# Expert layers over node columns split 250 and 376 instead of 312 and 314

## What is computed

```python
logits = jnp.einsum('td,ed->te', xf, gate_w)
probs = jax.nn.softmax(logits, axis=-1)
top_w, top_i = jax.lax.top_k(probs, TOP_K)
top_w = top_w / (top_w.sum(axis=-1, keepdims=True) + 1e-09)
combine = combine.at[jnp.arange(T)[:, None], top_i].add(top_w)
h = jax.nn.gelu(jnp.einsum('td,edh->teh', xf, w1) + b1[None, :, :])
y = jnp.einsum('teh,ehd->ted', h, w2) + b2[None, :, :]
out = jnp.einsum('ted,te->td', y, combine)
```

## Time and profile before

| | |
|---|---|
| median of 3 runs | 1740.7 us (1740.62 to 1742.16) |
| span of the profiled execution | 1740.0 us |
| TensorE busy | 1682.7 us, 97% |
| VectorE busy | 931.1 us, 54% |
| ScalarE busy | 466.8 us, 27% |
| GpSimd busy | 690.3 us, 40% |
| mean granted TensorE clock | 0.988 of full |

### The profile page before, as it was taken

How to read it: one execution, slowest core, us unless ns; L and a number is a source line. 1 busy time by engine, 2 the same in 40 slices (tenths; PEclk the granted TensorE clock), 3 DMA queues, 4 the chain that set the end, 5 groups by cost and what they waited for, 6 DMA issues and landing times.

```text
span 1740.0 us, 25810 instructions
## 1 busy us (share of the span) xinstructions
PE 1682.7 (97%) x10227; PEld 1579.9 (91%) x10227; DVE 931.1 (54%) x1879; ACT 466.8 (27%) x875; POOL 690.3 (40%) x428
## 2 busy tenths in 40 slices
PE   8799999999999988899999999999999999999999
PEld 7699999997999988799377888989999999998999
DVE  8993537416866679857497554423112141225731
ACT  6443123203223138934222211101011011112310
POOL 1026865652445520060020175431644435342663
PEclk9899999999999999899899999999999999999999
DMA  2002222423212210014010022111221111110222
GB/s 90 1 28 70 73 69 65 142 78 128 64 55 64 64 56 10 1 47 143 7 43 1 11 85 64 57 45 37 73 64 55 46 51 59 55 55 30 64 73 72
DMA packets 42000, 99.84 MB, mean 57 GB/s; under 512 B 10509, under 2 KB 12143, under 8 KB 41895
## 3 DMA queue, kind: packets, MB, share of 16 engines
q1 hardware_dynamic: 37828, 87.87, 16.3%
q10 hardware_dynamic: 4066, 10.46, 1.7%
HBM read 96.39 MB, written 1.92 MB: 57 GB/s over the span
## 4 chain that ended last, share of the span: by engine, by line
PE 82%; DVE 11%; ACT 4%; issue 1%; POOL 1%; DVEq 0%; POOLq 0%; ACTq 0%
PE bank L2421 10%; PE bank L2423 10%; PE bank L2422 10%; PE banks L2421 9%; PE banks L2422 9%; PE banks L2423 9%; PE bank L2983 3%; PE banks L2983 3%; PE bank L3060 3%; PE bank L3065 3%; PE banks L3060 2%; PE banks L3065 2%; DVE tmp L1827 1%; DVE src_hot L1491 1%; PE banks L2835 1%
## 5 line engine op out<-in xcount | busy, mean ns | idle before, releaser
L833 POOL TENSOR_TENSOR w_hi<-raw,ones_r 128x768 fp32r<-128x768 f32 (+1 forms) x192 | 294.0, 1532 | 994.9 <-PE banks L2423 368.3
L836 POOL TENSOR_TENSOR w_lo<-raw,w_hi 128x768 fp32r<-128x768 f32 (+1 forms) x192 | 370.5, 1930 | 15.0
L2421 PE MATMUL bank<-w_hi,xT_hi 128*125 128x384 f32 (+2 forms) x560 | 187.8, 335 | 1.7 <-DVE small L1968 1.2
L2423 PE MATMUL bank<-w_hi,xT_lo 128*125 128x384 f32 (+2 forms) x560 | 186.7, 333 | 0.0
L2422 PE MATMUL bank<-w_lo,xT_hi 128*125 128x384 f32 (+2 forms) x560 | 186.5, 333 | 0.0
L2421 PE MATMUL banks<-w_hi,xT_hi 128*125 128x384 f32 (+2 forms) x440 | 151.8, 345 | 0.2 <-DVE xT_lo L1569 0.2
L2422 PE MATMUL banks<-w_lo,xT_hi 128*125 128x384 f32 (+2 forms) x440 | 151.4, 344 | 0.0
L2423 PE MATMUL banks<-w_hi,xT_lo 128*125 128x384 f32 (+2 forms) x440 | 151.3, 344 | 0.0
L1618 DVE TENSOR_TENSOR hT_lo<-tmp,hT_hi 128x312 fp32r<-128x312 f32 (+1 forms) x88 | 94.3, 1078 | 41.9 <-ACT hT_hi L970 41.5
L2421 PEld LDWEIGHTS bank<-w_hi,xT_hi 128*125 128x125 f32 x560 | 103.9, 186 | 5.0 <-DVE small L1968 1.4
L2422 PEld LDWEIGHTS bank<-w_lo,xT_hi 128*125 128x125 f32 x560 | 103.9, 185 | 2.5
(11 more groups left out here) (579 smaller groups left out, 3923.4 us busy)
## 6 DMA issues: line engine op xcount, KB each, us to landing
raw<-wa SPq DMA_DIRECT2D x92, 384.0 KB, 3.0
raw<-wc SPq DMA_DIRECT2D x76, 384.0 KB, 3.0
raw<-wb SPq DMA_DIRECT2D x28, 448.0 KB, 3.3
w_rows<-w_in ACTq DMA_DIRECT2D x1, 3072.0 KB, 12.6
bias<-bias_in ACTq DMA_DIRECT2D x6, 384.0 KB
w_first<-w_in ACTq DMA_DIRECT2D x1, 2304.0 KB, 11.2
w_down<-w_down_in SPq DMA_DIRECT2D x8, 288.0 KB, 5.2
w_up<-w_up_in SPq DMA_DIRECT2D x1, 2304.0 KB, 10.6
```

Of the source, the lines that this page charges most:

```text
L833: pool.tensor_tensor(w_hi[:, k, 0:width], raw[:, k, 0:width], ones[:, 0:1].to_broadcast([P, width]), ALU.mult).then_inc(S("unit_high"), 1)
L836: pool.tensor_tensor(w_lo[:, k, 0:width], raw[:, k, 0:width], f(w_hi[:, k, 0:width]), ALU.subtract).then_inc(S("unit_split"), 1)
L2421: tell_used(pe.matmul(dst, l_hi, r_hi, start=start, stop=False))
L2423: return pe.matmul(dst, l_lo, r_hi, start=False, stop=stop)
```

## The change

The expert layers get their own split of the columns: part 0 has 250 (tiles 0 and 1), part 1 has 376. The first four jobs go in the order (tile 0, part 0), (tile 1, part 0), (tile 0, part 1), (tile 1, part 1); from job 4 on they are as before. The turn of tile 4 moves from ahead of job 0 to behind it. `router(0)` waits for the low parts of two tiles, not three. `router(1)` moves from behind job 0 to behind job 1, the transposes of the logits from behind job 1 to behind job 2, f1's importance from behind job 3 to behind job 4. The transposes of the routing weights stay behind job 5. As 376 columns are more than a slot of `tmp` holds, five slots of 376 lie in its place and a sixth behind `xT_hi`. The first product of the down layer waits for four low parts, not two. g0's up layer keeps 312 and 314.

```diff
+EXPERT_CH = [(0, 2 * TN), (2 * TN, NP - 2 * TN)]
...
-IMPORTANCE = 3
+IMPORTANCE = 4
+ROUTER_JOB = 1
...
     if s == "g0" and j < 6:
         return j % 3, j // 3
+    if s != "g0" and j < 4:
+        return j % 2, j // 2
     return j // 2, j % 2
+
+
+def columns_of(s, c):
+
+    return (CH if s == "g0" else EXPERT_CH)[c]
...
     def ffn(f, tiles):
         add(f + "_routerT", 0, f + "_routerT_read", 1)
-        left_turn()
         jobs, lag = 2 * tiles, EXPERT_LAG
         for j, spread in enumerate(spread_after(jobs)):
             if j < jobs:
                 add(f + "_hidden", j, f + "_activated", j + 1)
             if j == 0:
+                left_turn()
+            if j == ROUTER_JOB:
                 add(f + "_routerT", 1, f + "_routerT_read", 2)
-            if j == 1:
+            if j == ROUTER_JOB + 1:
                 add(f + "_router", 0, f + "_routed", 1)
...
+        last_slot = at_("last_slot", [P, EXPERT_CH[1][1]], f32, XT + up32(KD * NP * 4))
...
+        expert_tmp = at_("expert_tmp", [P, TSLOTS - 1, EXPERT_CH[1][1]], f32, tmp_off)
...
+        def slot_of(s, j, cn):
+
+            k = j % TSLOTS
+            if s == "g0":
+                return tmp[:, k, 0:cn]
+            return expert_tmp[:, k, 0:cn] if k < TSLOTS - 1 else last_slot[:, 0:cn]
...
                 def router(c):
-                    c0, cn = CH[c]
-                    pe.wait_ge(*E(s + "_xT_low", (6, 2 * NT)[c]))
+                    c0, cn = EXPERT_CH[c]
+                    pe.wait_ge(*E(s + "_xT_low", (4, 2 * NT)[c]))
...
                 router(0)
-                turn_behind(s)(NT - 1)
                 jobs = 2 * tiles
                 for j, spread in enumerate(spread_after(jobs)):
                     if j < jobs:
                         up(s, j)
                     if j == 0:
+                        turn_behind(s)(NT - 1)
+                    if j == ROUTER_JOB:
                         router(1)
-                    if j == 1:
+                    if j == ROUTER_JOB + 1:
                         pe.wait_ge(*E(s + "_routerT_read", 2))
...
-                down(s + "d", s + "_down", hT_hi, hT_lo, lambda k: pe.wait_ge(*E(s + "_low", 2 * k + 2)), seed=seed,
+                down(s + "d", s + "_down", hT_hi, hT_lo, lambda k: pe.wait_ge(*E(s + "_low", max(2 * k + 2, 4))), seed=seed,
```

More of the change, by code:

```diff
@@ L593, in network @@
         tmp = at_("tmp", [P, TSLOTS, WIDE], f32, tmp_off)
+        expert_tmp = at_("expert_tmp", [P, TSLOTS - 1, EXPERT_CH[1][1]], f32, tmp_off)
+        assert (TSLOTS - 1) * EXPERT_CH[1][1] <= TSLOTS * WIDE
         iota = new("iota", [TN, NP], i16)
@@ L967, in high @@
                     m, c = job_of(s, i)
-                    c0, cn = CH[c]
+                    c0, cn = columns_of(s, c)
                     act.wait_ge(*E(full, i + 1))
-                    act.activation(hT_hi[:, m, c0:c0 + cn], tmp[:, i % TSLOTS, 0:cn], ACT.Copy
+                    act.activation(hT_hi[:, m, c0:c0 + cn], slot_of(s, i, cn), ACT.Copy
                                    ).then_inc(S(s + "_high"), 1)
@@ L976, in hidden @@
                         m, c = job_of(s, j)
-                        cn = CH[c][1]
+                        cn = columns_of(s, c)[1]
                         if made <= j - TSLOTS:
@@ L983, in hidden @@
                             act.wait_ge(*E(s + "_low", j - TSLOTS + 1))
-                        act.activation(tmp[:, j % TSLOTS, 0:cn], bank(s + "_hidden", j)[:, 0:cn], func,
+                        act.activation(slot_of(s, j, cn), bank(s + "_hidden", j)[:, 0:cn], func,
                                        **scale_bias(m)).then_inc(S(s + "_activated"), 1)
@@ L992, in expert_layer @@
                 normal_rows(s)
-                for c, (c0, cn) in enumerate(CH):
+                for c, (c0, cn) in enumerate(EXPERT_CH):
                     await_group(act, s + "_routerT", c)
@@ L1607, in hidden_low @@
                     if j < jobs and weigh:
-                        cn = CH[j % 2][1]
+                        cn = columns_of(s, job_of(s, j)[1])[1]
                         dve.wait_ge(*E(s + "_activated", j + 1))
                         await_group(dve, s + "_cB", j)
-                        TT(tmp[:, j % TSLOTS, 0:cn], tmp[:, j % TSLOTS, 0:cn], bank(s + "_cB", j)[:, 0:cn], ALU.mult
+                        TT(slot_of(s, j, cn), slot_of(s, j, cn), bank(s + "_cB", j)[:, 0:cn], ALU.mult
                            ).then_inc(S(s + "_weighted"), 1)
@@ L1615, in hidden_low @@
                         m, c = job_of(s, i)
-                        c0, cn = CH[c]
+                        c0, cn = columns_of(s, c)
                         dve.wait_ge(*E(s + "_high", i + 1))
-                        TT(hT_lo[:, m, c0:c0 + cn], tmp[:, i % TSLOTS, 0:cn], f(hT_hi[:, m, c0:c0 + cn]),
+                        TT(hT_lo[:, m, c0:c0 + cn], slot_of(s, i, cn), f(hT_hi[:, m, c0:c0 + cn]),
                            ALU.subtract).then_inc(S(s + "_low"), 1)
@@ L2613, in expert_layer @@
                     for i in spread:
-                        m, (c0, cn) = i // 2, CH[i % 2]
+                        m, c = job_of(s, i)
+                        c0, cn = columns_of(s, c)
                         q, kind = (m // 3, m % 3) if tiles == 12 else (m // 2, 2 * (m % 2))
```

## The result

| | before | after |
|---|---|---|
| median of 12 runs each | 1742.12 us (1739.72 to 1745.59) | 1744.49 us (1743.62 to 1746.97) |
| ratio to before, with its 95% interval | | 1.0018 [1.0010, 1.0026] |
| span of the profiled execution | 1740.0 us | 1744.6 us |
| time of the profiled execution | about 1741.7 us (its span plus 1.7) | 1746.32 us |
| mean granted TensorE clock | 0.988 | 0.986 |

The change costs 0.18%: slower, but inside the 0.2% that was said to be no difference. The runs of before that stand beside it have a median 1.4 us above the three shown at first; a run's time is its span plus 1.7 us. The profiled execution of after is among its slower ones (1746.32 us, where the median is 1744.49), so its stretches can lie somewhat above those of the median execution.

What follows compares the result with a forecast made beforehand. TensorE, with a matmul in flight for 97% of the span, was taken as the bound. 1740.0 - 5.6 (entries) + 6.6 (routing) = 1741.0 us of span, plus 0.7 gives 1741.7 us; range 1734.5 to 1746.5.

Steps and rivals of the forecast that it cites:

- forecast case: Whole kernel: the summed gains and losses hold, 1741.7 us with its own range 1739.5 to 1744; chance 0.47.
- rival B: TensorE's clock falls behind f1's wait; job 5 at half clock loses 1.6 us: 1743.3, up to 1745; chance 0.2.
- likeliest case: Whole kernel: time within 0.2% (3.5 us) of before, between 1737.2 and 1744.2 us; chance 0.54.
- Columns: Up layers' products: 250 and 376 columns cost 287.5 ns a pair against 288.7 before; taken as 0 us.
- Rival C: fp32r products under 256 columns run at plain fp32's rate: 59 to 184 us more, 1800 to 1925; chance 0.07.
- terms for the cover: TensorE work between the logits' transposes and the routing weights' transposes: 9.05 us afterwards, 11.2 before.
- Entries: Expert layer entries: the router starts sooner, needing only two tiles; gains 0.95 (f0), 0.9 (f1), 3.8 (f3), 5.6 us in sum.
- Routing in f0 and f3: TensorE waits 1.85 us in each for the VectorE chain, which GpSimd's second split meets; bounds 1.4 and 2.4.
- f1's importance sum: In f1 TensorE waits 2.9 us for the probabilities ahead of this sum; bounds 0 and 3.5.
- part 3: Routing of f0, f1 and f3: shorter cover and GpSimd's burst cost 1.85 + 2.9 + 1.85 = 6.6 us.
- Rival A: GpSimd's burst misses the routing chain or small operations slip between; the 5.6 us gain stays: 1735 us; chance 0.22.
- Rival B's point of decision: In f1, the clock falls if the probabilities come over 2.5 us late.

Runs made afterwards that it cites:

- e1: The changed kernel with GpSimd splitting the fifth up-layer unit of all three expert layers only once the routing weights are written: 1739.07 us, ratio 0.9976.
- e5: The changed kernel with GpSimd's fifth-unit split held until the routing weights are written in f1 alone: 1739.29 us, ratio 0.9983.
- e4: The changed kernel's new order with the old 312 and 314 columns, the router's first half again waiting for three tiles: 1754.66 us, ratio 1.0068.
- e3: The changed kernel with the router's second half, logits' transposes and importance sum each one job earlier: 1744.39 us, ratio 1.0010.
- e2: The kernel before the change with GpSimd's fifth-unit split held until the routing weights are written in all three expert layers: 1743.0 us, ratio 1.0000.
- e6: The changed kernel's order with GpSimd's split held in all three expert layers, but the old 312 and 314 columns: 1742.23 us, ratio 1.0001.
- e7: Columns of 250 and 376 alone, with the order of jobs, turn and router of the kernel before: 1743.51 us, ratio 1.0005.
- e8: The changed kernel with f1's importance sum behind job 5 instead of job 4: 1743.79 us, ratio 1.0009.

## Why the prediction was right, and where it was off

The forecast was 1741.7 us of time, made from a profiled span plus 0.7 us; the median came out at 1744.49, beside 1742.12 for before. Against before that is +2.4 us where the sum had +1.0; the interval of the ratio is +1.7 to +4.5 us, and the three stretches of the profiled executions show +3.49. So the range of 1734.5 to 1746.5 holds the measured time, but the forecast case, which ended at 1744, does not quite, and what the trace shows is rival B. That no difference clear of 0.2% came out, as the likeliest case said, is in part luck: it is 0.18%.

- **Columns: right.** The starts of the router's products of 250 columns are 0.11 to 0.12 us apart (two of them in the first fence), and over the up jobs they are 117 ns (forecast 115.5) and 172 ns for 376 (forecast 172). The pair is 289 ns against 288.7. Rival C falls: 250 columns run on the line of the wider ones. (The prediction's 19 starts of 314 columns in 2.61 us are 145.0 ns apart, not 144.7, and its terms for the cover add up to 9.02, not 9.05; neither moves the sum by 0.1 us.)
- **Entries: right.** Gains 0.99, 1.02 and 3.73 us (forecast 0.95, 0.9 and 3.8), sum 5.7 against 5.6. The half clock near 1600 is gone, tile 4's rows cost f3 0.55 us (forecast 0.6), and TensorE waited for split weights at the same two places as before (190.9 and 616.3 us), none of them in these layers.
- **Routing in f0 and f3: right in kind, small in size.** The wait is 1.56 us each, forecast 1.85: the chain ended at T + 10.7, not 10.8, and TensorE came at T + 9.2, not 9.05. The burst of GpSimd hit exactly the two operations named. SBUF — State Buffer of the Trainium skill, Who interferes with whom, states that a VectorE instruction with two SBUF inputs contends with a GpSimd instruction that reads SBUF, and that a copy or cast can in a two-port mode. The rows of this case (three TENSOR_TENSORs and a cast that end 0.04 to 0.07 us behind GpSimd's instructions) and e1 (0.20 us instead of 1.41 and 1.78) agree with it.
- **f1's importance sum: the wait was right** (2.56 us, forecast 2.9, bounds 0 to 3.5), **the term was too small.** The step that failed is in the forecast's part 3, which priced f1 at the length of its wait and left the clock to rival B with a chance of 0.2 and 1.6 us. Rival B came true, and its own price was half of what the trace shows: the clock stayed at one half for 6.80 us, not 3.4, so 3.1 to 3.4 us on top of the wait. With it the sum of the terms is -5.7 + 1.56 + 2.56 + 1.56 + 3.1 to 3.4 = +3.1 to +3.4 us, and the stretches measured +3.49.
- **Rival A** (faster) falls: only L1667 slipped between two of GpSimd's instructions, and L1666 and L1668 were both held. It is what e1 makes true by hand, with 1739.07 us, not the 1735 of that rival.
- **Rival B's point of decision** was "over 2.5 us late"; the wait was 2.56. e5 and e1 show that the half clock hangs on the wait: without it, 1.00 in the whole window. The 2.5 itself is not borne out as a border. The half clock also follows waits of 1.99 and 1.97 us in e4 and one of 1.56 us in e3's f3, and does not follow the 1.56 us in f0 and f3 of after. What decides it stays open.

What is left between the stretches and the whole: after has 3.40 us of half clock from 653.9, in g2's attention, behind waits of 1.21 and 1.89 us for VectorE. Before, e2, e4, e5 and e6 don't have it; e1, e3, e7 and e8 do, within 6 us of there. The same two waits are there in before (1.18 and 1.89 us), with full clock. It costs half of that, 1.7 us, and comes and goes with edits that don't touch this code, so it is a scatter of that size on any comparison here. e1 is 3.6 us better than e5 in the stretches, but only 0.2 us in span (1737.3 against 1737.5) and, by the ratios, some 1.2 us in time. The traces show where the rest goes. When f0's stretch begins, e1 is already 0.89 us behind e5 (256.58 against 255.69), with 17.1 us of half clock so far where e5 has 13.7. Between f1's and f3's stretches it takes 2.36 us more, with two pieces of half clock of 3.40 us that e5 lacks, from 648.2 and from 689.2. What decides whether they come was not tried.

**The better version** is e1: the same columns and order, with GpSimd's fifth unit held until the routing is done, 0.24% under before. Against before the two intervals of e1 and e5 overlap, so which of the two is faster is not shown. Holding costs nothing on the weights' side: in f0 the split ends at 281.84, and TensorE needs the unit first in job 8, which starts at 285.50; no job of an expert layer waits for weights in e1.

## What to carry to other kernels

When a change shortens the way to a serial chain of small VectorE operations, look at what GpSimd does beneath that chain: here the split of one unit of weights stretched it by 2.5 us before the change and by 2.7 after, which cost nothing until the work that covered the chain got shorter. A wait put in front of that split, at no cost to its consumer, took the three stretches from 79.57 to 70.23 us and the ratio to before from 1.0018 to 0.9976. Price a new TensorE wait together with what the clock may do behind it, as a range: here the clock cost 3.1 to 3.4 us behind a wait of 2.56, nothing behind one of 2.49 (e4's f1), and about 1.7 behind one of 1.99 (e4's f0). And test an order and a size apart: here each was worth nothing or less without the other (e6, e7), and both together 5.9 us in the stretches once the chain was free.

## What the runs showed that was not expected

- The half clock lasted 3.40 us behind the entries and in e4 and e8, but 6.80 us behind f1's wait in after (and in three places that before has too, from 80.3, 705.0 and 834.7). What stood there was the wait of 2.56 us and then ten products of 8 columns each in 1.84 us; the clock fell 0.5 us after the first of them. In e8, with the tiny products ahead of the wait and full jobs behind it, it was 3.40.
- GpSimd takes a little longer beside VectorE as well: in e1 its split that starts at 278.21, while VectorE's cast of the bias (L1717) runs from 278.03 to 278.58, took 1.70 us instead of 1.47.
